# Two ScalarE copies of 400 elements per tile, and the modulation masks copied straight into the PSUM tile of the mask products

## The reference

```python
x = x + _L0_conv_ref(_gn(x), ...)    # binarised grouped 3x3 convolutions with batch norms
x = x + _L1_conv_ref(_gn(x), ...)    # deformable 3x3 convolution, 8 groups, 9 taps
```

```python
om = om_in.transpose(0, 2, 3, 1).reshape(n, L, c) @ om_w.T + om_b
off = om[..., :2 * K].reshape(n, h, w, G, K, 2) * OFFSET_SCALE
mask = om[..., 2 * K:]
out = jnp.einsum('nhwgk,nhwgkc->nhwgc', mask, sampled)
out = out.reshape(n, L, c) @ op_w.T
```

## Time and profile before

| | |
|---|---|
| median of 3 runs | 2926.51 us (2925.91 to 2933.81) |
| profiled execution | 2924.83 us, of which its span 2923.0 us |
| granted clock of TensorE, mean | 0.952 |
| busy: PE, DVE, ACT, POOL | 2430.8, 2205.6, 2259.7, 1917.6 us |
| instructions | 100581 |

### The profile page before, as it was taken

One profiled execution on the slowest core, in us unless ns is written; L12 is line 12 of the kernel. 1 busy time (PEld: TensorE's weight loads), 2 busy tenths in 40 slices (PEclk: granted clock), 3 DMA queues, 4 the chain that ended last, 5 costly groups with the idle time before them and its releaser, 6 DMA issues. The chain is left out here.

```text
span 2923.0 us, 100581 instructions
## 1 busy us (share of the span) xinstructions
PE 2430.8 (83%) x40456; PEld 2021.2 (69%) x40456; DVE 2205.6 (75%) x3095; ACT 2259.7 (77%) x4721; POOL 1917.6 (66%) x1452
## 2 busy tenths in 40 slices
PE   3999779993688888888888888888888888888887
PEld 2666556772577777777777777777777777777786
DVE  3555423334989897989888898989898988989773
ACT  2444256662989889898989898898989898989892
POOL 1000000003888888888988888888988898988892
PEclk8999889996899999999999999999999999999998
DMA  4555579975577677777777777777778777877675
GB/s 103 130 132 144 143 182 265 263 199 172 124 191 203 181 195 192 188 191 190 204 194 192 187 200 195 197 183 193 199 189 198 188 196 187 206 179 190 177 176 147
DMA packets 356164, 538.18 MB, mean 184 GB/s; under 512 B 171728, under 2 KB 258256, under 8 KB 355536
## 3 DMA queue, kind: packets, MB, share of 16 engines
q1 hardware_dynamic: 296656, 422.71, 60.3%
q10 hardware_dynamic: 59136, 110.11, 10.8%
HBM read 312.82 MB, written 219.77 MB: 182 GB/s over the span
## 5 line engine op out<-in xcount | busy, mean ns | idle before, releaser
L1109 ACT ACTIVATE dwt<-xp,wts 128x224 f32<-128x224 f32 x2016 | 797.3, 484 | 40.8 <-ACT wst L1135 31.8
L1280 PE MATMUL acc_p<-abuf,vbd 128*32 128x136 f32 (+5 forms) x20480 | 710.4, 291 | 54.9 <-issue 46.0
L1280 PEld LDWEIGHTS acc_p<-abuf,vbd 128*32 128x32 f32 (+1 forms) x20480 | 645.9, 145 | 117.7 <-issue 60.5
L979 DVE TENSOR_TENSOR pr<-mh_p,ht 128x864 f32<-128x864 f32 x672 | 668.9, 1051 | 23.2
L1258 PE MATMUL win_p<-pr,smat 128*128 128x160 f32 x4032 | 626.7, 310 | 27.3 <-POOL pr L1065 15.8
L246 PE MATMUL cv<-cin,wb 128*64 128x392 bf16 x6912 | 590.4, 333 | 25.8 <-ACT cin L225 25.8
L1258 PEld LDWEIGHTS win_p<-pr,smat 128*128 128x128 f32 x4032 | 570.4, 194 | 51.2 <-issue 22.4
L246 PEld LDWEIGHTS cv<-cin,wb 128*64 128x64 bf16 x6912 | 401.4, 110 | 208.7 <-ACT cin L225 25.9
L1048 POOL TENSOR_TENSOR dwt<-dwt 128x896 f32<-128x896 f32 x224 | 516.3, 2305 | 4.7 <-ACT dwt L1109 4.7
L1062 POOL TENSOR_TENSOR pr<-pr 128x576 f32<-128x576 f32 x224 | 317.3, 1417 | 187.8 <-DVE pr L979 187.8
L1135 ACT ACTIVATE wst<-win_p 128x200 f32<-128x200 f32 x896 | 388.6, 605 | 62.4 <-PE win_p L1258 38.7
(11 more groups left out here) (132 smaller groups left out, 2674.9 us busy)
## 6 DMA issues: line engine op xcount, KB each, us to landing
abuf<-weight_scratch SPq DMA_DIRECT2D x1568, 96.0 KB, 3.3
weight_scratch<-wst ACTq DMA_DIRECT2D x112, 960.0 KB, 6.2
xt<-x SPq DMA_DIRECT2D x128, 392.0 KB, 7.6
rows_scratch<-vsb SPq DMA_DIRECT2D x224, 128.0 KB, 2.1
vbd<-rows_scratch SPq DMA_DIRECT2D x896, 32.0 KB, 3.2
x_scratch<-xt SPq DMA_DIRECT2D x64, 392.0 KB, 6.6
y<-x SPq DMA_DIRECT2D x64, 392.0 KB, 4.4
x3h<-x_scratch SPq DMA_DIRECT2D x64, 392.0 KB, 4.9
```

The costliest lines, as they stand in the source:

```text
L979: dve.tensor_tensor(pr[:, j % 2, slots, :, :, :].rearrange("p k e x z -> p e k (x z)"), mh[:, a, :, :].rearrange("p (k x) z -> p k (x z)", ...
L1109: ins = act.activation(dwt[:, j % 2, k, :].rearrange("p (r w) -> p r w", w=W), image[:, r:r + BR, k % 3:k % 3 + W], ACT.Identity, scale=dw ...
L1280: mm = pe.matmul(acc_p[32 * (2 * s + b):32 * (2 * s + b) + 32, 0:2 * TN].rearrange("p (t w r) -> p t w r", t=BR, r=2)[:, t0:t1 + 1, x0:x1, :],
```

## The change

Three edits go together.

1. Layout. The columns of a slot are ordered half, group, row in place of half, row, group. The bias addition that copies `om_p` reads with the four rows (256 columns apart in `om_p`) innermost; its output is written in order as before.
2. Offsets and masks are copied apart. `copy_offsets` (576 elements) opens DVE's step and raises a new semaphore `off_ok`, for which ACT's hats now wait. `copy_masks` (288 elements) comes behind the three products and writes into the middle third of `mh_p`; it raises `om_ok`. `mask_hats` becomes two instructions: the outer two thirds of `mh_p` from the middle one and `ht` (576 elements), then, behind a wait on the first (`outer_ok`), the middle third by itself in place (288 elements). `oms` keeps the offsets only.
3. The five term slots of `win_p` lie without gaps (160 columns each, before 172 apart). The fourth then crosses from one PSUM bank (BANK = 512 columns) into the next, and its two matmuls are cut into 32 and 128 columns each. `copy_weights` makes two copies of 400 elements, one for even and one for odd rows, in runs of two; before, four copies of 200 in runs of four, each element of a run 480 elements from the next in `wst`.

```diff
-                def copy_om(i, j):
+                def offset_sums(i, j, to, lo, hi):
+                    return dve.tensor_tensor(
+                        to.rearrange("q w (g k) -> q (w g) k", k=BR),
+                        om_p[:, :].rearrange("q (k z) -> q z k", k=BR)[:, G * lo:G * hi, :],
+                        ombt[:, G * lo:G * hi].unsqueeze(2).broadcast_to([LANES, G * (hi - lo), BR]), ALU.add)
+
+                def copy_offsets(i, j):
                     dve.wait_ge(om_ready, NT * i + j + 1)
-                    dve.tensor_tensor(
-                        oms[:, j % 2, :, :].rearrange("q w (b k g) -> q (w b) k g", b=2, g=GS),
-                        om_p[:, :].rearrange("q (k z) -> q k z", k=BR)[:, :, 0:OMC].rearrange("q k (v g) -> q v k g", g=GS),
-                        ombt[:, :].rearrange("q (v g) -> q v g", g=GS).unsqueeze(2).broadcast_to([LANES, 6 * TAPS, BR, GS]),
-                        ALU.add).then_inc(om_ok, 1)
+                    offset_sums(i, j, oms[:, j % 2, :, :], 0, 2 * TAPS).then_inc(off_ok, 1)
+
+                def copy_masks(i, j):
+                    t = NT * i + j
+                    dve.wait_ge(om_ready, t + 1)
+                    wait(dve, pr_ok, 3 * t)
+                    offset_sums(i, j, mh[:, 1, :, :], 2 * TAPS, 3 * TAPS).then_inc(om_ok, 1)
 
                 def mask_hats(i, j):
-                    wait(dve, pr_ok, 3 * (NT * i + j))
-                    dve.wait_ge(hat_ok, NT * i + j + 1)
-                    dve.tensor_tensor(mh[:, :, :, :],
-                                      oms[:, j % 2, 2 * TAPS:3 * TAPS, :].unsqueeze(1).broadcast_to([LANES, 3, TAPS, BR * G]),
-                                      ht[:, j % 2, :, 0:TAPS, :], ALU.mult).then_inc(mh_ok, 1)
+                    t = NT * i + j
+                    dve.wait_ge(om_ok, t + 1)
+                    dve.wait_ge(hat_ok, t + 1)
+                    dve.tensor_tensor(mh[:, 0:3:2, :, :], mh[:, 1, :, :].unsqueeze(1).broadcast_to([LANES, 2, TAPS, BR * G]),
+                                      ht[:, j % 2, 0:3:2, 0:TAPS, :], ALU.mult).then_inc(outer_ok, 1)
+                    dve.wait_ge(outer_ok, t + 1)
+                    dve.tensor_tensor(mh[:, 1, :, :], mh[:, 1, :, :], ht[:, j % 2, 1, 0:TAPS, :], ALU.mult).then_inc(mh_ok, 1)
...
                     n = near(i, j, 2, first, last)
                     if n:
-                        copy_om(*n)
+                        copy_offsets(*n)
                     n = near(i, j, 1, first, last)
                     if n:
                         mask_hats(*n)
                         products(*n)
+                    n = near(i, j, 2, first, last)
+                    if n:
+                        copy_masks(*n)
...
-                    act.wait_ge(om_ok, t + 1)
+                    act.wait_ge(off_ok, t + 1)
...
-                    for k in range(BR):
-                        to = 2 * BR * (2 - 2 * (k % 2)) + BR * u + k
+                    for r in range(2):
+                        to = 4 * BR * (1 - r) + BR * u + r
                         cells = wst[:, 0, to:to + 1]
                         ins = act.activation(
-                            bass.AP(cells.tensor, cells.offset, [cells.ap[0], [PC, CT], [2 * BR, 2 * RT], [BAND, GS]]),
-                            win_p[:, 0:CT * WP].rearrange("p (e z) -> p e z", e=CT)[:, :, 0:RT * BR * G].rearrange(
-                                "p e (m k g) -> p e m k g", k=BR, g=GS)[:, :, :, k, :],
+                            bass.AP(cells.tensor, cells.offset, [cells.ap[0], [PC, GS * CT], [2 * BR, 2 * RT], [2, 2]]),
+                            win_p[:, 0:CT * RT * BR * G].rearrange("p (m g k r) -> p r g m k", g=GS, k=2, r=2)[:, r],
                             ACT.Copy)
...
-                        to = WP * e
+                        cuts = (0, 1, RT) if e == 3 else (0, RT)
                         for n, (a, b) in enumerate(terms):
-                            mm = pe.matmul(win_p[:, to:to + 160], smat[:, e, :],
-                                           pr[:, j % 2, 0:RT, a, b, :],
-                                           start=n == 0, stop=n == len(terms) - 1)
+                            for m0, m1 in zip(cuts, cuts[1:]):
+                                mm = pe.matmul(win_p[:, BR * G * (RT * e + m0):BR * G * (RT * e + m1)], smat[:, e, :],
+                                               pr[:, j % 2, m0:m1, a, b, :],
+                                               start=n == 0, stop=n == len(terms) - 1)
```

More of the change, by code:

```diff
@@ L61 @@
 RP = RT + 1
-WP = 172
 PC = 2 * BR * RP * 2
@@ L759, in l1_pass @@
         dwt = sb("dwt", [128, 2, TAPS, TN])
-        oms = sb("oms", [LANES, 2, 3 * TAPS, BR * G])
+        oms = sb("oms", [LANES, 2, 2 * TAPS, BR * G])
         ht = sb("ht", [LANES, 2, 3, 2 * TAPS, BR * G])
@@ L789, in l1_pass @@
         tap_ok, dw1_ok, dw2_ok, dw3_ok, dw_ok = map(sem, ("tap_ok", "dw1_ok", "dw2_ok", "dw3_ok", "dw_ok"))
-        om_ready, om_ok, abs_ok, far_ok, hat_ok, mh_ok, pr_ok, mg1_ok, mg_ok = map(sem, (
-            "om_ready", "om_ok", "abs_ok", "far_ok", "hat_ok", "mh_ok", "pr_ok", "mg1_ok", "mg_ok"))
+        om_ready, off_ok, om_ok, outer_ok, abs_ok, far_ok, hat_ok, mh_ok, pr_ok, mg1_ok, mg_ok = map(sem, (
+            "om_ready", "off_ok", "om_ok", "outer_ok", "abs_ok", "far_ok", "hat_ok", "mh_ok", "pr_ok", "mg1_ok", "mg_ok"))
         win_ok, wst_ok, amat_ok, accs_ok, misc_ready, misc_ok, carried, passed = map(sem, (
@@ L1019, in _ @@
                     read_misc(j + 1, value=(0, j))
-                for j in range(2):
-                    copy_om(0, j)
+                copy_offsets(0, 0)
+                copy_masks(0, 0)
+                copy_offsets(0, 1)
                 mask_hats(0, 0)
                 products(0, 0)
+                copy_masks(0, 1)
                 for j in range(NT):
@@ L1115, in hats @@
                     t, u = NT * i + j, j % 2
-                    off = oms[:, u, 0:2 * TAPS, :]
+                    off = oms[:, u, :, :]
                     wait(act, pr_ok, 3 * (t - 1))
-                    act.wait_ge(om_ok, t + 1)
+                    act.wait_ge(off_ok, t + 1)
                     act.activation(ht[:, u, 1, :, :], off, ACT.Abs).then_inc(abs_ok, 1)
```

## The result

The changed kernel takes 2981.95 us (2974.28 to 2990.76), the kernel before beside it 2926.21 us: a ratio of 1.0184 [1.0167, 1.0202], slower by 56 us. That is clear of the noise, if not clearly under or over 2%, and 51 us above the forecast of 2931, inside the range given (2880 to 2985). The profiled execution took 2974.28 us, the least of four, and 49.5 us more than that of before (2924.83).

The account below looks back on a forecast made before the run. DVE's length was taken to count in seven of fourteen steps, the DVE-PE chain in the others. Terms 55.8 + 14.1 + 54.2 + 11.3 = 135.4 a pair, plus 0.3 for stalls, gave 2931 us; range 2880 to 2985, forecast's own 2905 to 2957.

Parts of the forecast that it names:

- The loop: Without input sums, masks' copy releases PE's misc block, which releases DVE's output add: a closed loop of 9.04 us.
- quiet steps: Steps 4 and 9 to 13 of a pair's 14, without input sums: about 9.0 us each, DVE waiting some 2.5.
- Step 8: Step behind step 7's double input sum, PE at a lowered clock: 11.27 us against 6.55 before.
- summing steps: Steps 0 to 3, 5 and 6, where DVE also sums the next pair's input: 9.30 us against 9.96.
- step 7: Step of a pair with a double input sum on DVE: 14.11 us against 14.77, a gain of 0.66.
- slow reads: Rival: DVE's two copies read om_p slowly at a step of 256 elements; up to 0.95 us a step, 3144; chance 0.12.
- dearer PSUM source: Rival: each of DVE's two mask products costs 0.04 us more reading PSUM; 2949 us; chance 0.05.
- L920 and the masks' copy: Input sum's start on DVE: the masks' copy falls into a wait for POOL, delaying L920's end by 0.10 at most.
- rival of longer copies: ACT's weight copies take 1.5 us each, two 3.0, setting steps 9 to 13; 3090 us; chance 0.04.
- The cut: PE's term slot 3 matmuls, eight records for four: 0 to 0.6 us a step, covered by PE's 0.9 in hand.
- The stalls: PE's pauses before the weighted sums: about 3 us a pair, 1.0 each, mostly fitting PE's 0.9; 0.3 a pair added.
- rival of the full gain: PE keeps its clock at step 8 and no stall reaches DVE: 2883 us; chance 0.25.

Follow-up runs that it names:

- a quarter of the weight write: Three quarters of ACT's weight write to DRAM left out: 2935.84 us in the changed kernel, 2925.00 us in the kernel before.
- DVE's part: Changed kernel with four ScalarE copies, nine uncut window matmuls and term slots 172 columns apart again; DVE's edits stay: 2962.01 us.
- `om_ok` ahead: Changed kernel with PE's misc block reordered (value rows and projection first, offset rows last), the wait for om_ok back at its head: 2962.61 us.
- ScalarE's and PE's part: Changed kernel with DVE's single copy, single mask product and early om_ok restored; layout, cut matmuls and two ScalarE copies stay: 2935.28 us.
- `dw_ok` ahead: PE's misc block reordered (offset rows last), the wait for dw_ok back at its head: changed kernel 2868.89 us, kernel before 2921.83 us.

## Why the prediction was right or wrong

- **The loop: right.** DVE waits 2.52 us in quiet steps (forecast some 2.5), the step is 8.92 us (9.04), PE is released by the masks' copy 156 times from 700 to 2700 us. Step 8 is 11.50 (11.27), summing steps 9.13 (9.30). What they are shorter by lies mostly in the waits on the instruction just before: 0.11 was put down for each, but only the one ahead of the products takes 0.10, the other two 0.03. In step 7 the gain of 0.7 did not come in the median, 14.85 against 14.8 before; with a quarter of the weight write it did (14.17). In the changed kernel DVE waits up to 1.8 us there for the loads of the input sum, 7 times from 700 to 2700 us, a wait that the forecast did not have.
- **The DVE instructions: right.** 0.76, 0.47, 0.75 and 0.47 us for a forecast of 0.77, 0.46, 0.77 and 0.46. The rivals of slow reads and of a dearer PSUM source fall with these rows. By the estimate from the Trainium skill (VectorE: DVE Perf Modes, the section on the TRN2 errata) each mask product would be 0.06 longer; the trace shows no such excess.
- **The mask product without its slow cases: right.** The Trainium skill (SBUF — State Buffer, "Who interferes with whom") says that a VectorE instruction with two SBUF inputs contends with a GpSimd instruction that reads SBUF, and that one with at most one such input, outside the modes that use two ports, doesn't. The trace agrees, from both sides: the product with the masks from PSUM takes a steady 0.75 (0.74 to 0.85 over all 224), and POOL's addition of 448 elements falls from a mean of 1.49 to 1.19 us.
- **L920 and the masks' copy: right.** The first part of the input sum takes 0.62 where it took 1.03: the masks' copy lies in what the prediction had read as a wait for POOL.
- **ScalarE: right.** The copies take 0.53 each, and nothing was gained by them with the old order. The rival of longer copies falls with that; its "1.3 more than four now" was a slip besides, since two copies of 1.5 are 3.0 against four of 0.60, 0.6 more.
- **The cut: inside its bounds**, 0.35 of 0 to 0.6; but "PE's 0.9 covers either" was too kind. PE's remaining wait is 0.48 us behind the longer weighted sums, and the cut alone cost 7.5 us in the kernel before, where PE had stood still for 1.05 us ahead of its block.
- **The stalls: the step that failed.** The prediction took 3 us of pauses a pair, 1.0 each, from the earlier trace rows, let them "mostly fit" into 0.9 us of reserve, and added 0.3 a pair with ends of 0 and 1. Three things were wrong. The group counts the weighted sums alone and an average: pauses of over 2 us, which no reserve of 0.9 takes up, were there before too, and the windows have pauses of their own. The pauses were taken to stay as they were: those of over 2 us in the weighted sums are 4 before and 16 after. And a long pause brings the clock down: behind the one shown the windows were 1.67 us longer, behind another of 3.7 us 0.85. The earlier trace rows had shown that for step 8, and the stalls were not given the same.
- **What the stalls cost.** Measured, the disturbances cost 4.1 us a pair (mean against median; before 1.1) where the forecast had 0.3, and the undisturbed steps were 0.9 shorter than forecast: 138.6 against 135.7 is 2.9 a pair, 46 us in 16 pairs, where the profiled execution lies 43 above the forecast; the median of the runs is 8 us more.
- **How far the loop is to blame.** That the wait for `om_ok` makes the loss is shown by putting it alone back to the block's head, at 88 us, pauses included. That the closed loop passes on more of a pause is shown in part: per pair, the steps with pauses and those behind them are longer by 38% to 84% of the pauses in four closed kernels (the changed one, DVE's part, a quarter of the write, `om_ok` ahead) and by 25% to 44% in four open ones (before, before with a quarter of the write, the cut, ScalarE's and PE's part), one profile of each; the shares overlap.
- **The range: luck.** It holds the 2982, but its upper end of 2985 stood for a quarter of the slow reads, which did not come; the forecast's own range ended at 2957, and none of the slower rivals had the pauses.
- **What the earlier trace rows left unnamed.** PE's 1.05 us ahead of L1195 was taken as a gap in a chain between DVE and PE. It was the wait for POOL's depthwise rows, as the run with `dw_ok` ahead and POOL's row above show. The forecast of the changed kernel did not depend on it, but whoever had asked what ended it would have seen that the block's head holds two waits which most of the block does not need.
- **The rival of the full gain** (2883): its time is reached, but behind another edit and not by its condition. With the offset rows last the changed kernel takes 2869 to 2875 us, 1.8% to 1.9% under the kernel before, though PE's rows in step 8 are still slow (3.14 us in place of 1.68); the output add just does not wait for them. In the changed kernel itself the granted clock in the step 8 shown was 0.50 over 4.0 us (1522.5 to 1526.5), lower than the 0.64 of the earlier trace rows.

## What to carry to other kernels

An added wait that closes a chain to a loop has two prices: the loop's own length, which rows give well, and the disturbances inside it, of which it seems to absorb less; cost the long ones and what follows them (here the clock), not their average, and allow for their becoming more. Where a wait stands at the head of a block, ask which instructions of the block need it: moving the others ahead of it was worth 24 us to the kernel before and 107 us to the changed one. Two edits that shorten two engines can be worth nothing each and 29 us together, so try the second on top of the first before dropping it.

## What the runs showed of the hardware

- PE can stand still for up to 3.9 us within a long run of matmuls that waits for no semaphore; in 39 of the 42 cases over 0.5 us in the changed kernel it started again 1.1 to 1.9 us, mostly some 1.4, after a packet of instructions had landed.
- After a pause of 3.45 us PE's granted clock over the next 4.8 us was 0.64, and 22 window records took 4.73 us in place of 3.06.
- ScalarE writes 400 elements in runs of two in 0.53 us, where 200 elements, each 480 apart from the next in a run, took 0.60: the pattern cost more than the count. In the run with DVE's part alone, which reads in another pattern and writes as before, they also took 0.60, so it is not the reading. DVE reads PSUM with a step of 256 elements at no loss (576 elements in 0.76 us).
